# Loading, summing and storing the results by token tile on two DMA queues

## The reference

```python
x = x + jnp.tanh(g_xattn[0]) * _L0_xattn_ref(ctx_1024, ctx_1024, _layernorm(x, axis=-1), ...)
x = x + jnp.tanh(g_ffn[0]) * _L0_ffn_ref(_layernorm(x, axis=-1), ...)
# inside _L0_ffn_ref, with TOP_K = 2:
topk_probs, topk_idx = jax.lax.top_k(probs, TOP_K)
...
out = jnp.sum(y * topk_probs[..., None], axis=-2)
```

## Time and profile before

| | |
|---|---|
| three runs | 112.81, 113.01, 113.17 us (median 113.01) |
| the profiled execution's own time | 113.34 us |
| its span from first to last instruction | 111.6 us |
| mean granted TensorE clock | 0.814 of full speed |
| busy: PE, DVE, ACT, POOL | 65%, 47%, 45%, 48% of the span |
| last scatter issued / landed | 100.12 / about 102.24 us |
| loads of the results issued | 102.26 to 104.29 us |
| sums on DVE and POOL | 105.31 to 109.33 us |
| stores issued | 106.22 to 109.73 us |

### The profile page before, as it was taken

The page is one execution under the profiler, slowest core; times in us unless marked ns, Lnnn a source line. Parts: engine busy times, 40 slices in busy tenths (PEclk is TensorE's granted clock), DMA queues, the critical chain, the costliest instruction groups (busy, mean ns, idle before and its releaser), DMA issues.

```text
span 111.6 us, 2488 instructions
## 1 busy us (share of the span) xinstructions
PE 72.3 (65%) x707; PEld 61.9 (55%) x707; DVE 52.6 (47%) x222; ACT 50.1 (45%) x155; POOL 53.4 (48%) x79
## 2 busy tenths in 40 slices
PE   5667955774664200570599999999999999920000
PEld 2256823554454200210399999999999999910000
DVE  1377855499978728309812332433134213310261
ACT  4122387689676600600056654754577277600000
POOL 6668501133677777760000547454755366472050
PEclk9999999996555555569557999999999999995555
DMA  2999980000010123720553453011010111000954
GB/s 49 321 435 405 452 356 15 6 3 3 24 48 24 48 69 90 179 72 24 121 121 86 117 145 72 22 27 47 7 53 24 34 35 32 23 0 0 267 161 136
DMA packets 10748, 11.57 MB, mean 104 GB/s; under 512 B 1491, under 2 KB 9703, under 8 KB 10480
## 3 DMA queue, kind: packets, MB, share of 16 engines
q1 hardware_dynamic: 8768, 8.69, 24.3%
q0 software_dynamic: 1248, 2.12, 6.1%
q10 hardware_dynamic: 720, 0.62, 2.0%
HBM read 8.18 MB, written 3.70 MB: 106 GB/s over the span
## 4 chain that ended last, share of the span: by engine, by line
PE 37%; issue 32%; DMA 10%; POOL 7%; SPq 6%; DVE 5%
PE bank L676 18%; PE bank L664 5%; PE bank L666 5%; PE bank L665 5%; SPq L278 3%; DMA res<-results 3%; DMA wp<-in_wpack 3%; PE bank L653 3%; POOL results L391 3%; POOL x_bias L369 2%; DMA results<-y_sb,in_rows 2%; DMA in_rows<-dispatched 2%; POOL rstd L360 2%; DVE out_sb L916 1%; DVE stats L727 1%
## 5 line engine op out<-in xcount | busy, mean ns | idle before, releaser
L513 ACT ACTIVATE hid<-bank,wp 128x128 f32<-128x128 f32 x92 | 25.5, 376 | 24.7 <-PE bank L666 15.4
L391 POOL DMA_INDIRECT results<-y_sb,in_rows x23 | 22.6, 983 | 28.5 <-DVE y_sb L899 25.6
L676 PE MATMUL bank<-w_sb,hid 128*128 x184 | 25.4, 282 | 0.0
L676 PEld LDWEIGHTS bank<-w_sb,hid 128*128 128x128 f32 x184 | 22.5, 192 | 0.1
L324 POOL DMA_INDIRECT dispatched<-rows,slot x16 | 15.8, 987 | 5.1 <-issue 4.2
L664 PE MATMUL bank<-xs_t,w_hi 128*128 128x128 f16 x92 | 18.1, 231 | 0.1
L665 PE MATMUL bank<-xs_t,w_hi 128*128 128x128 f16 x92 | 18.2, 231 | 0.0
L666 PE MATMUL bank<-xs_t,w_lo 128*128 128x128 f16 x92 | 18.2, 231 | 0.0
L895 DVE COPY xs_t<-bank 128x256 f16<-128x256 f16 x23 | 6.6, 289 | 18.0 <-PE bank L653 13.2
L899 DVE TENSOR_SCALAR y_sb<-bank,in_rows 128x128 f32<-128x128 f32 x23 | 8.0, 349 | 12.9 <-PE bank L676 10.6
L522 PE MATMUL bank<-ones 128*128 128x512 bf16 x14 | 6.3, 627 | 8.9 <-issue 7.7
(11 more groups left out here) (132 smaller groups left out, 120.5 us busy)
## 6 DMA issues: line engine op xcount, KB each, us to landing
w_sb<-in_w SPq DMA_DIRECT2D x2, 2048.0 KB, 11.5
in_rows<-dispatched SPq DMA_DIRECT2D x23, 65.0 KB, 2.0
res<-results SPq DMA_DIRECT2D x4, 256.0 KB, 3.7
ctx_sb<-in_ctx_t SPq DMA_DIRECT2D x1, 512.0 KB, 5.5
out<-out_sb SPq DMA_DIRECT2D x4, 128.0 KB, 1.8
results<-y_sb,in_rows POOLq DMA_INDIRECT x23
wp<-in_wpack ACTq DMA_DIRECT2D x1, 342.0 KB, 3.8
dispatched<-pad_rows SPq DMA_DIRECT2D x5, 65.0 KB, 5.2
```

The costliest lines, as they stand in the source:

```text
L391: pool.indirect_dma_start(results_dram, bass.IndirectOffsetOnAxis(ap=in_rows[:].bitcast(U32)[:, t, TARGET:TARGET + 1], axis=0), y_sb[:, t, ...
L513: mm = act.activation(hid[:, t % HIDS, b, :], hid_ps[t % HID_PS][:, b * P:(b + 1) * P], ACT.Gelu_apprx_tanh, bias=b1[:, bass.ds(experts[t] ...
L676: mm = pe.matmul(to, hid[:, t % HIDS, b, :], w2_sb[:, bass.ds(e, 1), b * P:(b + 1) * P], start=False, stop=b == BLOCKS - 1)
```

## The change

The four chunks of two tiles go. Each of the 8 token tiles has its own load (128 KB), semaphore, pair of additions of 128 x 128, and store (64 KB). SP issues the loads and stores of tiles 0, 2, 4 and 6, and ACT those of tiles 1, 3, 5 and 7, after a wait of its own for `scattered`. Each queue issues its four loads and then its four stores, each store behind a wait for its tile's sum. POOL sums tiles 2 and 6, DVE the other six in order (0, 1, 3, 4, 5, 7). SP's last wait is for all 8 stores.

```diff
-        chunks = [slice(2 * i, 2 * i + 2) for i in range(4)]
-        POOL_CHUNK = 1
+        POOL_TILES = (2, 6)
+        DVE_TILES = tuple(t for t in range(TILES) if t not in POOL_TILES)
...
+        def load_results(queue, first):
+
+            queue.wait_ge(scattered, 16 * N_TILES)
+            for t in range(first, TILES, 2):
+                queue.dma_start(res[:, t, :, :], res_view[:, t, :, :]).then_inc(ld_res[t], 16)
+
+        def store_sums(queue, first):
+
+            for t in range(first, TILES, 2):
+                if t in POOL_TILES:
+                    queue.wait_ge(pool_out_ok, POOL_TILES.index(t) + 1)
+                else:
+                    queue.wait_ge(out_ok, DVE_TILES.index(t) + 1)
+                queue.dma_start(out_view[:, t, :], out_sb[:, t, :]).then_inc(stored, 16)
...
-            sp.wait_ge(scattered, 16 * N_TILES)
-            for i, q in enumerate(chunks):
-                sp.dma_start(res[:, q, :, :], res_view[:, q, :, :]).then_inc(ld_res[i], 16)
-            for i, q in enumerate(chunks):
-                if i == POOL_CHUNK:
-                    sp.wait_ge(pool_out_ok, 1)
-                else:
-                    sp.wait_ge(out_ok, i + 1 - (i > POOL_CHUNK))
-                sp.dma_start(out_view[:, q, :], out_sb[:, q, :]).then_inc(stored, 16)
-            sp.wait_ge(stored, 16 * len(chunks))
+            load_results(sp, 0)
+            store_sums(sp, 0)
+            sp.wait_ge(stored, 16 * TILES)
...
-            q = chunks[POOL_CHUNK]
-            pool.wait_ge(ld_res[POOL_CHUNK], 16)
-            pool.tensor_tensor(out_sb[:, q, :], res[:, q, 0, :], neg_x1[:, q, :], ALU.subtract).then_inc(pool_summed, 1)
-            pool.wait_ge(pool_summed, 1)
-            pool.tensor_tensor(out_sb[:, q, :], out_sb[:, q, :], res[:, q, 1, :], ALU.add).then_inc(pool_out_ok, 1)
+            for i, t in enumerate(POOL_TILES):
+                pool.wait_ge(ld_res[t], 16)
+                pool.tensor_tensor(out_sb[:, t, :], res[:, t, 0, :], neg_x1[:, t, :], ALU.subtract).then_inc(pool_summed, 1)
+                pool.wait_ge(pool_summed, i + 1)
+                pool.tensor_tensor(out_sb[:, t, :], out_sb[:, t, :], res[:, t, 1, :], ALU.add).then_inc(pool_out_ok, 1)
...
+            load_results(act, 1)
+            store_sums(act, 1)
...
-            for i, q in enumerate(chunks):
-                if i != POOL_CHUNK:
-                    v.wait_ge(ld_res[i], 16)
-                    n = then(v.tensor_tensor(out_sb[:, q, :], res[:, q, 0, :], neg_x1[:, q, :], ALU.subtract))
-                    v.wait_ge(dve, n)
-                    v.tensor_tensor(out_sb[:, q, :], out_sb[:, q, :], res[:, q, 1, :], ALU.add).then_inc(out_ok, 1)
+            for t in DVE_TILES:
+                v.wait_ge(ld_res[t], 16)
+                n = then(v.tensor_tensor(out_sb[:, t, :], res[:, t, 0, :], neg_x1[:, t, :], ALU.subtract))
+                v.wait_ge(dve, n)
+                v.tensor_tensor(out_sb[:, t, :], out_sb[:, t, :], res[:, t, 1, :], ALU.add).then_inc(out_ok, 1)
```

More of the change, by code:

```diff
@@ L245, in gated_block @@
         scattered = sem("scattered")
-        ld_res, out_ok, pool_summed, pool_out_ok, stored = [sem(f"ld_res{i}") for i in range(len(chunks))], sem("out_ok"), sem("pool_summed"), sem("pool_out_ok"), sem("stored")
+        ld_res, out_ok, pool_summed, pool_out_ok, stored = [sem(f"ld_res{t}") for t in range(TILES)], sem("out_ok"), sem("pool_summed"), sem("pool_out_ok"), sem("stored")
         x_view = x.rearrange("(t p) d -> p t d", p=P)
```

## The result

The changed kernel took 114.45 us (median of four runs, 114.27 to 115.13) against 112.91 us of the kernel before (four runs, 112.62 to 113.17). The ratio is 1.0148, with a 95% interval from 1.0097 to 1.0199: 1.5 us slower, where 0.2 us faster was forecast and 113.6 was the end of the range. Its profiled execution took 114.3 us, with a span of 112.6.

A forecast was written before the change was run, and what follows sets the result against it. DVE was to bound the tail from the first landing on. From the profiled 113.34 us, -0.02 at DVE's end and -0.20 at the store gave 113.12, and 0.33 less for the median gave 112.8 us; range 112.0 to 113.6.

The forecast's parts named there:

- 2.65 in the sum: Start of DVE's first sum in the tail: first landing taken as 2.6 us, plus a wake of 0.05.
- where 0.20 was taken: Last store, now one tile of 64 KB: 0.2 us gained after DVE's end (bounds 0 and 0.3).
- the part on DVE's end: Tail: landing 104.86, wake 0.05, work 3.20, holds 1.20 put DVE's end at 109.31, where it had been 109.33.
- so it isn't last: POOL's sums of tile 6: begun near 107.7, ended by 109.2 at the latest, so POOL would not set the end.
- For this sum DVE must never wait for data: DVE's sums in the tail: each tile lands before DVE comes to it, tiles 4 and 5 by 107.1.
- hold no load up: 0: Early stores in the tail travel behind their own queue's loads and cost the loads 0 us.
- the holds: POOL's four additions in the tail each hold DVE for 0.30 us, 1.20 in all (bounds 0 and 1.80).
- The slower one: Rival: DVE's chain in the tail runs from a first landing no earlier than before; 113.4 to 114.0 us, chance 0.25.
- The one by which the two queues share the DMA engines: Mechanism in the slower rival: the first pair of tiles shares the DMA engines, tile 0 lands at 105.26 as chunk 0 did.

The follow-up runs named there:

- e3: Kernel before, with a wait for DVE's last sum and then a one-column memset added on POOL: ratio 1.0134, tail 10.7 us.
- e4: Kernel before, with only a wait for DVE's last sum added on POOL, no operation behind it: ratio 1.0121, tail 10.8 us.
- e1: Changed kernel with all eight tiles summed by DVE, none by POOL: ratio to the kernel before 1.012, tail 9.8 us.
- e2: Changed kernel with POOL summing tiles 2 and 3 instead of 2 and 6: ratio to the kernel before 0.9994, tail 9.2 us.
- e6: Changed kernel with all sums on DVE and both queues waiting for all eight loads before their first store: ratio to the kernel before 1.0078, tail 9.6 us.
- e10: As e9, but with the stores issued by ACT: tail 9.3 us, no ratio (two runs).
- e9: Changed kernel with all loads and stores on SP's queue and all sums on DVE: ratio to the kernel before 1.0043, tail 9.4 us.
- e7: Kernel before, its four chunks kept, with chunks 1 and 3 loaded and stored by ACT: ratio 1.012 (two runs), tail 10.1 us.
- e12: Changed kernel with all loads and stores on SP's queue and POOL summing only tile 1: ratio to the kernel before 0.9966, tail 9.5 us.

## Why the prediction was wrong, point by point

**What was right.** The issues ran side by side, 0.38 to 0.49 us each. The first sum began at 2.57, against 2.65 in the sum (2.6 and a wake of 0.05). Additions of 128 x 128 took 0.29 us on DVE and 0.45 on POOL, and DVE's period for a tile was 0.54 (104.22 to 104.76), against 0.52. The last stores of 64 KB landed in 1.6 us:

```profile
out<-out_sb SPq DMA_DIRECT2D x2, 64.0 KB, 1.6
out<-out_sb ACTq DMA_DIRECT2D x2, 64.0 KB, 1.6
```

From DVE's end to SP's branch it took 1.71 us instead of 1.90, a gain of 0.19 where 0.20 was taken.

**The step that failed: "so it isn't last".** In the part on DVE's end I followed POOL to the end of its last addition, found it earlier than DVE's, and dropped it. What counts is that end plus 3.28 us until its DRAIN is through. By the forecast's own latest time for it, 109.2, the DRAIN would have ended at 112.5, and the span with it 0.23 later at 112.7, 1.1 above the span before. The measured end of POOL came 0.44 later still, at 7.38 instead of 6.94 into the tail, since its sums of tile 6 began at 6.26 and not near 5.4; the two make up the 1.56. The row was in the trace of the kernel before (POOL's DRAIN from 107.0, 4.04 us), and it had 0.15 us to spare; I read the chain and the waits, where it doesn't appear, because the stores came last. In the changed kernel it is 1.3 of the 1.56 us: without it the tail would have ended 0.36 after SP's branch, at 9.6. The other 0.26 is DVE's end, 0.46 later, less what the smaller stores gave. e3 and e4 show the mechanism in the kernel before, and in the changed one e1 shows the tail without it, e2 with it 1.7 us earlier.

**The second step that failed: "For this sum DVE must never wait for data".** Tiles 4 and 5 were to land by 107.1, 4.8 into the tail. DVE waited 0.69 us for tile 4 and began it at 5.40. Why it landed late stays open. The prediction's "hold no load up: 0" for the early stores is a suspect: in e1 DVE began tile 4 0.83 us later than in e6, where stores were held. But in e2 it began it at 4.42 with stores as early, and e10 against e9 gives 0.24 us for one tile and nothing for the one before. Two stores of 64 KB at the 300 GB/s of the earlier trace rows are some 0.4 us by my estimate, less than the 1 us between the changed kernel and e2. So the bytes of the stores alone don't explain it, and the spread of the landings from one execution to the next is of the same size as the effect.

**A size that was off: the holds.** Four holds of 0.30 gave 1.20. DVE's four additions beside POOL took 0.40, 0.50, 0.54 and 0.49 us, so 0.77 above 0.29 in all. It goes the other way too, which no row of before had shown: POOL's first additions took 0.49 and 0.60 where DVE was ahead, 0.45 otherwise. This 0.43 less didn't pay for the waits: 0.69 us for tile 4, another 0.13 for tile 3 (begun at 105.42, where 105.29 would follow from the period between tiles 0 and 1 without a hold), and 0.08, the overlap of one tile's last addition with the next tile's first (104.55 + 0.29 against 104.76) that a wait takes away. DVE's end came out at 7.53 instead of 7.05.

**The rivals.** The slower one named DVE's chain, with a price of up to 1 us. DVE's end did come 0.46 later than before, but from a first landing that was early, so the sign was right for another reason. The one by which the two queues share the DMA engines is true for large loads (4.00 in e7) and much smaller for tiles (2.27 to 2.65 against 2.10 to 2.18 on one queue). The Trainium skill says so ("DMA: Bandwidth & Descriptors", section "Issuing engines are not separate DMA queues"): transfers interleave on the same engines, and only issue time is saved. The runs agree with it, the gain in issue time included: eight issues on one queue spread over 3.97 us, four on each of two over 2.02. e7 goes beyond it: the last load landed 0.5 us later than on one queue (6.1 against 5.7 into the tail) with the same bytes, and no run shows why.

## What to carry to other kernels

An engine's last operation is not its end: look at the DRAIN of each engine at the end of the program, POOL's above all, and add it to the path of every engine that the change makes later, even by a trivial operation or a wait. Give POOL the work that comes first in the last stage, or none; late work on it must end some 3.3 us before the last store has landed. In e2, and on one queue in e9 and e12, the tail was back at 9.2 to 9.5 us by that; no run here shows a gain over the kernel before. And judge the landing of loads by more than one profile: the same loads with the same early stores let DVE begin tile 4 at 5.4 and 5.6 in two executions, and at 4.4 in a third.

## What the runs showed of the hardware

- POOL's DRAIN at the end of the program is through 3.26 to 3.28 us after its last operation or wait, whatever that was: 3.28 after an addition in both kernels, 3.27 after a memset (e3), 3.26 after a wait alone (e4), 3.27 after the last scatter (e1). DVE's took 0.33 to 0.53 us from its start and ACT's 0.15 to 0.88. That POOL also issues indirect transfers in this kernel may be part of it; no run here leaves them out.
- Additions of DVE and POOL with two inputs in SBUF hold each other, whichever comes second: in the changed kernel DVE by 0.11 to 0.25 us for an operation of 0.29, POOL by up to 0.15 for one of 0.45.
- Of two loads of 256 KB issued side by side on two queues the first landed after 4.0 us (e7), where one after the other on one queue it landed after 3.0; a load of 128 KB landed first after 2.1 to 2.2 us on one queue and 2.3 to 2.6 on two.
- The end of the program follows the last store by 0.36 us after SP's branch, or POOL's DRAIN by 0.23 us, whichever is later, in all fourteen profiles.
